# One-core decoder layer: the experts' gates multiply the input rows, and the second product runs in two-part form into one PSUM sum

## The chip, the core and the metric

The kernel runs on one core of a Trainium2 chip. The metric is the time of one execution on the device, in microseconds (us). Engines are named as in the profile: PE (TensorE, with PEld for its weight loads), DVE (VectorE), ACT (ScalarE), POOL (GpSimd) and SP (SyncE, which issues most transfers).

## The reference

One decoder layer on x of shape (4, 256, 128), in three parts, each added to x. Self attention has 16 heads and a causal mask, on 8 sequences of 128 in its own setup (here 4 of 256). Cross attention has 16 heads of 8 on a context of 4 x 256 rows. The part that changes is the mixture of 8 experts, of which each row uses 2:

```
scores = x @ Wr + br                     # 128 -> 8, x is the layer-normalised row
weights = softmax over the best two scores, 0 elsewhere
for i in range(8):
    h = relu(xi @ W1[i] + b1[i])         # 128 -> 512, xi = x where expert i is chosen, else 0
    out += (h @ W2[i] + b2[i]) * weights[..., i:i+1]    # 512 -> 128
```

## The kernel before

**Order.** A table `slots` is written out once in Python. Each engine walks it and emits its own part of every unit, so one row of the table sets the order on all engines, and semaphores do the rest. Every engine works strictly in that order: a wait in one unit holds back all later units of that engine.

**Stages.** First the self attention (`S`, `T`, `V`, `Z`). Then the cross attention: for each batch b of four, eight slots g with two score products (`CS`), whose exponentials ACT writes (`cross_probabilities`, L930), and the value products (`CO`, L718). Beside them run the maxima that a later batch needs (`MX` on PE L682, reduced on DVE L1128), their turn and stacking (`mT`, `stack_m`), and the way out of the batch before (`oq0`, `oT0`, `oq1`, `oT1`, `wo`). All of these small steps share PSUM bank 7 and go one after another. In the slots of batch 2 stands also `WS`: ACT rounds one expert's first weights to fp32r (`weight_high`, L948), and DVE writes the remainder (`weight_low`, L1157).

**Experts.** The 1024 rows go in two halves of 512, and each half meets 8 experts, so there are 16 periods k. In each, PE forms the hidden values in four chunks (`H`, helper `products`, L530 to L532): a product of fp32 accuracy in two-part form, high x high, low x high, high x low, three fp32r products of 512 columns. ACT and DVE take turns in adding the bias b1, applying relu and writing `hid` in fp32 (L953 and L1201). Then `Y` (`combine`, L792) forms the second product of the period before with plain fp32 products: 4 groups of 128 rows x 4 chunks, `hid` being the stationary operand and `w2` the moving one with 128 columns. DVE multiplies each result by the row's gate and adds it to `resid` (`accumulate`, L1220). `NT`, `RT`, `GT`, `WT`, `B2` are the turn of the normalised rows, the router's scores, the gates, their turn and the bias b2.

**Transfers.** SP issues the expert weights in the cross stage: w1 (L389), the stacked maxima of batch 2 (`stack_m(2)`, six small transfers), w2 (L392), then `stack_m(3)`. They all go through one queue.

## Time and profile before

| | |
|---|---|
| Runs | 337.38, 337.92, 335.69 us; median 337.38 us |
| Profiled execution | 336.25 us, of which the span is 334.5 us |
| Busy share of the span | PE 92%, DVE 58%, ACT 49%, POOL 20% |
| Mean granted TensorE clock | 0.995 |
| Last quarter of the cross attention with batch 2 and 3 | 189.8 to 220.6 us |
| Experts | 220.6 to 330.6 us |

The page's shares are means over stages that differ. A PE record's duration includes the time in which the next product already runs, so the price of a product in a stream is the distance between starts.

### The profile page before, as it was taken

To read this page: it belongs to the slowest core of one execution; us is meant where nothing else is said; L and a number is where in the kernel's file an instruction comes from. 1 tells how busy PE (TensorE), PEld (TensorE's weight loads), DVE (VectorE), ACT (ScalarE), POOL (GpSimd) and SP (SyncE) were. 2 spreads that over 40 slices of the span, in tenths; PEclk is the share of its full clock that TensorE was granted. 3 is DMA by queue.
4 is the path that set the end of the run, shared out by engine and by line. 5 is a ranking of instruction groups with operands and counts; after the bars stand their busy time and mean duration, and the time that the engine had idled before them with its cause. 6 is when DMAs were issued, how large, how long until landed. Compare 5 with 4: busy or idle time off the path is not lost.

```text
span 334.5 us, 5887 instructions
## 1 busy us (share of the span) xinstructions
PE 306.4 (92%) x2177; PEld 230.3 (69%) x2194; DVE 193.5 (58%) x450; ACT 163.4 (49%) x466; POOL 66.3 (20%) x102
## 2 busy tenths in 40 slices
PE   6789999999989898889687879899999999999995
PEld 2577677867866676556334333378999988998995
DVE  3677565457297875772877883363553564434432
ACT  1679767487646663663565778742212121212210
POOL 7991470301031003620300203020020000000000
PEclk9999999999999999999999997999999999999999
DMA  8800025511000100010016720000000001000001
GB/s 237 199 2 1 3 39 66 64 21 35 15 2 0 39 11 1 3 29 23 1 35 230 213 81 3 2 2 0 2 0 2 0 3 32 0 2 0 2 0 31
DMA packets 13884, 11.98 MB, mean 36 GB/s; under 512 B 2616, under 2 KB 10912, under 8 KB 13856
## 3 DMA queue, kind: packets, MB, share of 16 engines
q1 hardware_dynamic: 12272, 10.81, 13.6%
q10 hardware_dynamic: 1584, 0.80, 0.9%
q8 instruction: 17, 0.28, 0.4%
q14 instruction: 11, 0.09, 0.1%
HBM read 7.84 MB, written 0.52 MB: 25 GB/s over the span
## 4 chain that ended last, share of the span: by engine, by line
PE 76%; DVE 15%; issue 3%; ACT 3%; POOL 2%; DMA 1%; another core or an unknown queue 0%; DVEq 0%; ACTq 0%; POOLq 0%
PE ps L792 17%; PE ps L530 7%; PE ps L531 7%; PE ps L532 7%; PE ps L604 6%; PE ps L637 5%; PE ps L649 4%; DVE mneg L1128 4%; PE ps L682 4%; PE ps L718 4%; PE ps L703 3%; PE ps L611 2%; PE ps L639 2%; DVE negmax L1097 2%; DVE t_lo L1063 2%
## 5 line engine op out<-in xcount | busy, mean ns | idle before, releaser
L901 ACT ACTIVATE p<-ps,negmax 128x256 f32<-128x256 f32 (+1 forms) x128 | 52.6, 425 | 25.4 <-DVE negmax L1097 24.9
L792 PEld LDWEIGHTS ps<-w_raw,hid 128*128 128x128 f32 x512 | 59.5, 192 | 1.3
L792 PE MATMUL ps<-w_raw,hid 128*128 128x128 f32 x512 | 59.6, 275 | 0.0
L953 ACT ACTIVATE hid<-ps,b1T 128x512 f32<-128x512 f32 x32 | 21.9, 687 | 73.9 <-PE ps L532 73.9
L1128 DVE TENSOR_REDUCE mneg<-ps 128x2 f32<-128x512 f32 x64 | 42.1, 682 | 14.0 <-PE ps L682 13.3
L1097 DVE TENSOR_REDUCE negmax<-ps 128x2 f32<-128x512 f32 (+1 forms) x48 | 32.9, 686 | 19.6 <-PE ps L606 12.4
L930 ACT ACTIVATE px<-ps 128x512 f32<-128x512 f32 x64 | 35.3, 600 | 18.1 <-PE ps L703 15.1
L1220 DVE SCALAR_TENSOR_TENSOR resid<-ps,wgt,resid 128x128 f32<-128x128 f32 x64 | 18.0, 344 | 42.9 <-PE ps L792 42.9
L682 PE MATMUL ps<-k_st,q_mem 128*128 128x256 bf16 x128 | 24.7, 276 | 9.4 <-DVE mneg L1128 8.7
L1201 DVE TENSOR_SCALAR hid<-ps,b1T 128x512 f32<-128x512 f32 x32 | 23.8, 749 | 11.0 <-PE ps L532 10.9
L424 POOL TENSOR_SCALAR tmp<-mv 128x2 f32<-128x2 f32 x8 | 2.1, 268 | 141.2 <-DVE mv L1121 141.2
L887 ACT CAST t_hi<-ps 128x512 fp32r<-128x512 f32 x32 | 18.7, 591 | 19.6 <-PE ps L532 18.7
L530 PE MATMUL ps<-n_parts,w_hi 128*128 128x512 f32 x64 | 27.6, 431 | 0.0
L901 ACT ACTIVATION_READ_ACCUMULATOR p<-ps,negmax 128x1 f32 x128 | 26.6, 208 | 0.0
L532 PE MATMUL ps<-n_parts,w_hi 128*128 128x512 f32 x64 | 25.3, 396 | 0.0
L531 PE MATMUL ps<-n_parts,w_lo 128*128 128x512 f32 x64 | 25.3, 395 | 0.0
L682 PEld LDWEIGHTS ps<-k_st,q_mem 128*128 128x128 bf16 x128 | 9.4, 97 | 21.3 <-DVE mneg L1128 16.8
L604 PE MATMUL ps<-t_hi,n_parts 128*128 128x512 f32 x64 | 23.1, 441 | 0.3 <-DVE t_lo L1063 0.3
L1063 DVE TENSOR_TENSOR t_lo<-ps,t_hi 128x512 fp32r<-128x512 f32 x32 | 21.4, 681 | 1.9 <-ACT t_hi L887 1.9
L703 PE MATMUL ps<-q_mem,k_st 128*128 128x512 bf16 x56 | 20.4, 398 | 0.3 <-ACT px L930 0.2
L530 PE MATMUL ps<-n_parts,g_hi 128*128 128x256 f32 x64 | 20.6, 322 | 0.0
L637 PE MATMUL ps<-p,v_sb 128*64 128x256 f32 x128 | 20.1, 392 | 0.4 <-DVE v_sb L1109 0.4
...
## 6 DMA issues: line engine op xcount, KB each, us to landing
w_raw<-in_L_ffn_W SPq DMA_DIRECT2D x1, 2048.0 KB, 8.5
...
p<-in_L_attn_W_o SPq DMA_DIRECT2D x1, 512.0 KB, 8.0
p<-in_ctx SPq DMA_DIRECT2D x1, 512.0 KB, 9.2
```

The lines of the kernel that those rows point to most:

```text
L530: pe.matmul(out, a[0], b_[0], start=True, stop=False)
L531: pe.matmul(out, a[1], b_[0], start=False, stop=False)
L532: return pe.matmul(out, a[0], b_[1], start=False, stop=True)
L604: pe.matmul(bank, n_parts[:, a, S * b:S * b + P], t_ring[t][:, 2 * (u % 6):2 * (u % 6) + 2, :], start=(a + t == 0), stop=False)
L637: last = pe.matmul(o, v, p0[:, h, :], start=True, stop=False)
L682: last = pe.matmul(ps[:, max_bank[("MX", b, u)], S * par:S * par + S], q_st[b][:, g, S * par + P * qt:S * par + P * qt + P], k_st[:, g, S ...
L703: pe.matmul(ps[:, k % 3, :], k_st[:, g, S * b + P * kt:S * b + P * kt + P], q_st[b][:, g, :], start=True, stop=True).then_inc(s_st, 1)
L792: last = pe.matmul(ps[:, Y_BANK[k % 2], P * tt:P * tt + P], hid[:, k % 2, c, P * tt:P * tt + P], w2_sb[:, NC * e + c, :], start=(c == 0), ...
L901: last = act.activation(dst, bank[:, n * i:n * i + n], ACT.Exp, bias=negmax[:, kt, h:h + 1], accum_out=psums[:, kt, h:h + 1])
L930: act.activation(px[:, (g // 2) % 2, c0:c0 + 512], ps[:, k % 3, :], ACT.Exp, scale=SCALE_X).then_inc(s_px, 1)
L1097: dve.tensor_reduce(dst, ps[:, k % 3, :].rearrange("p (h q) -> p h q", h=n), AX, ALU.max, negate=True).then_inc(s_max, 1)
L1128: dve.tensor_reduce(mneg[:, qt, :].rearrange("p (r g) -> p r g", r=2)[:, :, g], ps[:, max_bank[("MX", b, u)], :].rearrange("p (h k) -> p h ...
```

## The change

The gate is at least 0, so gate x relu(x W1 + b1) = relu((gate x) W1 + gate b1). The changed kernel multiplies the input rows by the gate instead of the result:

- `X` (`gate_rows`) is a new PE product that spreads the gate of expert e over 128 partitions. DVE multiplies the turned rows `nT` by it (`gated`), ACT writes the high part (`gated_high`), DVE the low part (`gated_low`). It stands one period ahead: `X` of k+1 opens the slot of period k.
- The biases b1 and br go into the last row of the weights: a normalised row sums to 0, so its last element is replaced by 1 and the last weight row is subtracted from the others. POOL does so for w1 (`first_weights`, 8 pieces), and it needs `w1_last`, the last row of every expert's w1 repeated on all partitions (2 MB in SBUF), and b1 must land in row 127 of w1 after w1 did. `weight_high` now waits for both.
- All four relu chunks go through ACT (high part) and then DVE (low part).
- `Y` has the weights as stationary operand and moves 512 rows, in two-part form: 4 chunks x 3 fp32r products, and all experts of a half sum up in one PSUM bank. `accumulate` is gone. The sum is copied by ACT (`YE`), turned by PE (`YO`) and added to `resid` by DVE (`finish_rows`), and the output leaves in four parts, not two.
- w2 is split too: ACT writes the high part (`second_high`), POOL the low part (`second_weights`).
- b2 is one product per half. `NT`, `RT`, `GT`, `WT` and `X` of the first half stand in the slots of batch 3 of the cross attention, where before `NT` and `RT` did.

On ACT, in the cross stage, this is the first stretch with `WS` before (p and px are probabilities, w_hi the rounded weights, oT and m_f small steps):

```order
L939 COPY o_raw<-ps 128x512 [waits s_pv]
L948 CAST w_hi<-w_raw 128x512 [waits s_w1]
L930 ACTIVATE px<-ps 128x512 [waits s_pv,s_st] x2
L964 COPY b1T<-ps 128x32 [waits s_misc]
L948 CAST w_hi<-w_raw 128x512 [waits s_w1]
L930 ACTIVATE px<-ps 128x512 [waits s_pv,s_st] x2
```

and now:

```order
L1025 COPY o_raw<-ps 128x512 [waits s_pv]
L1035 CAST w_hi<-w_raw 128x512 [waits s_b1,s_wdiff]
L1016 ACTIVATE px<-ps 128x512 [waits s_pv,s_st] x2
L1035 CAST w_hi<-w_raw 128x512 [waits s_b1,s_wdiff]
L1016 ACTIVATE px<-ps 128x512 [waits s_pv,s_st] x2
```

The place is the same, the wait is another: for b1's transfer and POOL's difference. Later on ACT, in batch 3, stands a new wait for the router's scores:

```order
L1060 COPY nT<-ps 128x512 [waits s_misc]
L1016 ACTIVATE px<-ps 128x512 [waits s_pv,s_st] x2
L1057 ACTIVATE gate<-gate 128x4 [waits s_score]
L1016 ACTIVATE px<-ps 128x512 [waits s_pv,s_st] x4
L1029 COPY oT<-ps 128x128 [waits s_misc]
```

On SP the transfers of the experts now stand so (m_part are the stacked maxima, of batch 2 and then of batch 3):

```order
L409 DMA w_raw<-in_L_ffn_W 128x8x512 [waits s_misc]
L411 DMA w_last<-in_L_ffn_W 128x8x512
L415 DMA b_sb<-in_L_ffn_b 8x128 [waits s_zero]
L415 DMA b_sb<-in_L_ffn_b 8x128
L398 DMA q_mem<-m_part 1x8x256 [waits s_mpart]
L398 DMA q_mem<-m_part 1x8x256 x5
L417 DMA w_raw<-in_L_ffn_W 128x32x128
L419 DMA w_raw<-in_L_ffn_b 1x4096 [waits s_w1]
L398 DMA q_mem<-m_part 1x8x256 [waits s_mpart]
```

The broadcast (L411) is new between w1 and the maxima, and b1 (L419) stands behind w2. The diff, cut to its core:

```diff
-            more = {(2, 1): [("b1", 0)], (3, 1): [("NT", 0)], (3, 7): [("RT", 0)]}
+            more = {(3, 0): [("NT", 0)], (3, 1): [("RT", 0)], (3, 3): [("GT", 0), ("W2", 0, 0)], (3, 5): [("W2", 0, 1)],
+                    (3, 6): [("WT", 0)], (3, 7): [("X", 0)]}
...
-        extra = {0: [("GT", 0), ("oq0", last)], 1: [("WT", 0), ("oT0", last)], 2: [("B2", 0), ("oq1", last)], 3: [("oT1", last), ("wo", last)],
-                 5: [("NT", 1)], 6: [("RT", 1)], 7: [("GT", 1)], 8: [("WT", 1)], 9: [("B2", 1)]}
+        beside = {(0, 0): [("oq0", last)], (0, 1): [("oT0", last)], (0, 2): [("oq1", last)], (0, 3): [("oT1", last)],
+                  (1, 0): [("wo", last)], (3, 1): [("NT", 1)], (4, 0): [("RT", 1)], (5, 1): [("GT", 1)],
+                  (6, 3): [("WT", 1)], (9, 0): [("YO", 0, 0)], (9, 1): [("YO", 0, 1)]}
         for k in range(2 * NE):
-            more = extra.get(k, []) + [None, None]
-            units = [("H", k, 0), more[0], ("H", k, 1), ("H", k, 2), more[1], ("H", k, 3)]
-            slots.append([u for u in units if u] + ([("Y", k - 1)] if k else []))
-        slots.append([("Y", 2 * NE - 1)])
-        MISC = ("PJ", "n2T", "q", "mT", "oq0", "oT0", "oq1", "oT1", "wo", "b1", "NT", "RT", "WT", "B2")
+            slot = [("YE", 0, 0), ("YE", 0, 1)] if k == NE + 1 else []
+            slot += [("X", k + 1)] if k + 1 < 2 * NE else []
+            for c in range(NC):
+                slot += [("H", k, c)] + beside.get((k, c), [])
+            if k + 2 < NE:
+                slot += [("W2", 0, k + 2)]
+            if k % NE == 2:
+                slot += [("B2", k // NE)]
+            slots.append(slot + ([("Y", k - 1)] if k else []))
+        slots.append([("Y", 2 * NE - 1), ("YE", 1, 0), ("YE", 1, 1), ("YO", 1, 0), ("YO", 1, 1)])
...
+        X_BANK = 6
...
-        G_BANK, H_BANK, Y_BANK = (0, 1, 2, 7), (0, 1, 2, 5), (6, 3)
+        G_BANK, H_BANK, Y_BANK = (0, 1, 2, 7), (0, 1, 2, 5), (3, 4)
...
-            sp.dma_start(b1_nat[:, :], b1.rearrange("e (c p) -> (e c) p", p=P)).then_inc(s_ffnb, 16)
...
             sp.dma_start(w1_raw[:, :].rearrange("p (e n) -> p e n", n=HID), w1.rearrange("e p n -> p e n")
                          ).then_inc(s_w12[0], 16)
+            sp.dma_start(w1_last[:, :].rearrange("p (e n) -> p e n", n=HID), w1[:, LAST, :].partition_broadcast(P)
+                         ).then_inc(s_wlast, 16)
+            sp.wait_ge(s_zero, 1)
+            for r in (0, LOW):
+                sp.dma_start(b2_sb[r:r + NE, :], b2).then_inc(s_b2, 16)
             stack_m(2)
-            sp.dma_start(w2_sb, w2.rearrange("e (c p) d -> p (e c) d", p=P)).then_inc(s_w12[1], 16)
+            sp.dma_start(w2_raw[:, :].rearrange("p (n d) -> p n d", d=D), w2.rearrange("e (c p) d -> p (e c) d", p=P)).then_inc(s_w12[1], 16)
+            sp.wait_ge(s_w12[0], 16)
+            sp.dma_start(w1_raw[LAST:D, :], b1.rearrange("e n -> (e n)").unsqueeze(0)).then_inc(s_b1, 16)
             stack_m(3)
...
-                sp.wait_ge(s_acc, NE * (hf + 1))
-                sp.dma_start(out.rearrange(tiles, p=P)[:, 4 * hf:4 * hf + 4, :],
-                             resid[:, 4 * hf:4 * hf + 4, :]).then_inc(s_out, 16)
-            sp.wait_ge(s_out, 32)
+                for i in range(2):
+                    ts = slice(4 * hf + 2 * i, 4 * hf + 2 * i + 2)
+                    sp.wait_ge(s_misc_ev, misc_at[("YO", hf, i)] + 1)
+                    sp.dma_start(out.rearrange(tiles, p=P)[:, ts, :], resid[:, ts, :]).then_inc(s_out, 16)
...
+            def first_weights(i):
+                if i == 0:
+                    pool.wait_ge(s_w12[0], 16)
+                    pool.wait_ge(s_wlast, 16)
+                cols = slice(512 * i, 512 * i + 512)
+                pool.tensor_tensor(w1_raw[0:LAST, cols], w1_raw[0:LAST, cols], w1_last[0:LAST, cols], ALU.subtract
+                                   ).then_inc(s_wdiff, 1)
+            def second_weights(i):
+                pool.wait_ge(s_w2hi, i + 1)
+                cols = slice(512 * i, 512 * i + 512)
+                pool.tensor_tensor(w2_lo[:, cols], w2_raw[:, cols], w2_hi[:, cols].bitcast(F32), ALU.subtract
+                                   ).then_inc(s_w2lo, 1)
...
+            for i in range(NE):
+                first_weights(i)
             norm_3(0)
             norm_3(1)
             norm_3(2)
+            for i in range(3):
+                second_weights(i)
             norm_3(3)
+            for i in range(3, NE):
+                second_weights(i)
...
                 elif kind == "RT":
+                    pe.wait_ge(s_pick, 3)
                     for t in ts:
-                        for i in range(2):
-                            last = pe.matmul(ps[:, 7, NE * (t % 4):NE * (t % 4) + NE],
-                                             n_parts[:, i, P * t:P * t + P].bitcast(F32), wr_sb[:, :],
-                                             start=(i == 0), stop=(i == 1))
+                        last = pe.matmul(ps[:, 7, NE * (t % 4):NE * (t % 4) + NE], nT[:, P * t:P * t + P], wr_sb[:, :],
+                                         start=True, stop=True)
...
+            def gate_rows(k):
+                e, hf = k % NE, k // NE
+                if k == 0:
+                    pe.wait_ge(s_mx_ev, 16 * B)
+                if e == 0:
+                    pe.wait_ge(s_misc_ev, misc_at[("WT", hf)] + 1)
+                ge(pe, s_xf, k)
+                pe.matmul(ps[:, X_BANK, :], pick[:, e, :], wgtT[:, 512 * hf:512 * hf + 512], start=True, stop=True
+                          ).then_inc(s_gt, 1)
             def hidden(k, c):
-                e, hf = k % NE, k // NE
+                e = k % NE
                 if k == 0 and c == 0:
                     pe.wait_ge(s_wlo, 8)
                     pe.wait_ge(s_px, 16 * B)
                     pe.wait_ge(s_mx_ev, 16 * B)
-                if k % NE == 0 and c == 0:
-                    pe.wait_ge(s_misc_ev, misc_at[("NT", hf)] + 1)
+                if c == 0:
+                    pe.wait_ge(s_xlo, k + 1)
                 if k >= 1:
-                    pe.wait_ge(s_ha if c % 2 == 0 else s_hd, 2 * (k - 1) + c // 2 + 1)
-                products(ps[:, H_BANK[c], :], [w[:, e, P * c:P * c + P] for w in w1_p], n_of(512 * hf, 512)).then_inc(s_h, 1)
+                    pe.wait_ge(s_hd, 4 * (k - 1) + c + 1)
+                products(ps[:, H_BANK[c], :], [w[:, e, P * c:P * c + P] for w in w1_p],
+                         [x[:, k % 2, :] for x in x_p]).then_inc(s_h, 1)
             def combine(k):
-                e = k % NE
+                e, hf = k % NE, k // NE
+                out_bank = ps[:, Y_BANK[hf], :]
+                pe.wait_ge(s_w2lo, e + 1)
                 if k == 0:
-                    pe.wait_ge(s_w12[1], 16)
                     pe.wait_ge(s_pv_ev, 2 * B)
-                ge(pe, s_acc, k - 1)
-                pe.wait_ge(s_ha, 2 * k + 2)
-                pe.wait_ge(s_hd, 2 * k + 2)
-                for tt in range(4):
-                    for c in range(NC):
-                        last = pe.matmul(ps[:, Y_BANK[k % 2], P * tt:P * tt + P], hid[:, k % 2, c, P * tt:P * tt + P],
-                                         w2_sb[:, NC * e + c, :], start=(c == 0), stop=(c == NC - 1))
+                for c in range(NC):
+                    pe.wait_ge(s_hd, 4 * k + c + 1)
+                    w, h = [w[:, NC * e + c, :] for w in w2_p], [x[:, k % 2, c, :] for x in hid]
+                    pe.matmul(out_bank, w[0], h[0], start=(e == 0 and c == 0), stop=False)
+                    pe.matmul(out_bank, w[1], h[0], start=False, stop=False)
+                    last = pe.matmul(out_bank, w[0], h[1], start=False, stop=(e == NE - 1 and c == NC - 1))
                 last.then_inc(s_y, 1)
+            def second_bias(hf):
+                pe.wait_ge(s_b2, 32)
+                pe.matmul(ps[:, Y_BANK[hf], :], b2_sb[:, :], wgtT[:, 512 * hf:512 * hf + 512].bitcast(F32),
+                          start=False, stop=False)
...
             def weight_high(i):
-                act.wait_ge(s_w12[0], 16)
+                act.wait_ge(s_wdiff, i + 1)
+                act.wait_ge(s_b1, 16)
                 act.copy(w1_hi[:, 512 * i:512 * i + 512], w1_raw[:, 512 * i:512 * i + 512]).then_inc(s_whi, 1)
-            def relu(k, c):
+            def second_high(i):
+                act.wait_ge(s_w12[1], 16)
+                act.wait_ge(s_wdiff, NE)
+                act.copy(w2_hi[:, 512 * i:512 * i + 512], w2_raw[:, 512 * i:512 * i + 512]).then_inc(s_w2hi, 1)
+            def gated_high(k):
+                act.wait_ge(s_xf, k + 1)
+                ge(act, s_h, 4 * (k - 1))
+                act.copy(x_p[0][:, k % 2, :], x_f[:, k % 2, :]).then_inc(s_xhi, 1)
+            def relu_high(k, c):
                 act.wait_ge(s_h, 4 * k + c + 1)
                 ge(act, s_y, k - 1)
-                act.activation(hid[:, k % 2, c, :], ps[:, H_BANK[c], :], ACT.Relu,
-                               bias=b1T[:, NC * (k % NE) + c:NC * (k % NE) + c + 1]).then_inc(s_ha, 1)
-            def expert_copy(kind, hf):
+                act.activation(hid[0][:, k % 2, c, :], ps[:, H_BANK[c], :], ACT.Relu).then_inc(s_ha, 1)
...
+                    act.wait_ge(s_y, NE * (hf + 1))
+                    ge(act, s_misc, misc_at[("YO", hf - 1, i)] + 1 if hf else 0)
+                    half_cols = slice(S * i, S * i + S)
+                    act.copy(yT[:, half_cols], ps[:, Y_BANK[hf], half_cols]).then_inc(s_yT, 1)
...
-            def relu(k, c):
-                dve.wait_ge(s_h, 4 * k + c + 1)
-                ge(dve, s_y, k - 1)
-                dve.tensor_scalar(hid[:, k % 2, c, :], ps[:, H_BANK[c], :], b1T[:, NC * (k % NE) + c:NC * (k % NE) + c + 1],
-                                  0.0, ALU.add, ALU.max).then_inc(s_hd, 1)
...
+            def gated(k):
+                hf = k // NE
+                dve.wait_ge(s_gt, k + 1)
+                ge(dve, s_xhi, k - 1)
+                dve.tensor_tensor(x_f[:, k % 2, :], ps[:, X_BANK, :], nT[:, 512 * hf:512 * hf + 512], ALU.mult
+                                  ).then_inc(s_xf, 1)
+            def gated_low(k):
+                dve.wait_ge(s_xhi, k + 1)
+                dve.tensor_tensor(x_p[1][:, k % 2, :], x_f[:, k % 2, :], x_p[0][:, k % 2, :].bitcast(F32), ALU.subtract
+                                  ).then_inc(s_xlo, 1)
+            def relu_low(k, c):
+                dve.wait_ge(s_ha, 4 * k + c + 1)
+                dve.scalar_tensor_tensor(hid[1][:, k % 2, c, :], ps[:, H_BANK[c], :], 0.0,
+                                         hid[0][:, k % 2, c, :].bitcast(F32), ALU.max, ALU.subtract).then_inc(s_hd, 1)
+            def finish_rows(hf, i):
+                dve.wait_ge(s_misc, misc_at[("YO", hf, i)] + 1)
                 dve.wait_ge(s_n3, 4 * hf + 4)
-                ge(dve, s_acc, accumulated(hf))
-                dve.tensor_tensor(resid[:, ts, :], ps[:, 7, :].rearrange("p (t d) -> p t d", d=D),
+                ts = slice(4 * hf + 2 * i, 4 * hf + 2 * i + 2)
+                dve.tensor_tensor(resid[:, ts, :], ps[:, turn_bank(hf, i), 0:S].rearrange("p (t d) -> p t d", d=D),
                                   resid[:, ts, :], ALU.add).then_inc(s_misc_ev, 1)
-                dve.wait_ge(s_misc_ev, misc_at[("B2", hf)] + 1)
-            def accumulate(k):
-                e, hf = k % NE, k // NE
-                dve.wait_ge(s_y, k + 1)
-                dve.wait_ge(s_n3, 4 * hf + 4)
-                ge(dve, s_acc, k)
-                for tt in range(4):
-                    t = 4 * hf + tt
-                    last = dve.scalar_tensor_tensor(resid[:, t, :], ps[:, Y_BANK[k % 2], P * tt:P * tt + P],
-                                                    wgt[:, t, e:e + 1], resid[:, t, :], ALU.mult, ALU.add)
-                last.then_inc(s_acc, 1)
...
+                    elif kind == "H":
+                        relu_low(b, *i)
+                        if i[0] == 0 and b + 1 < 2 * NE:
+                            gated_low(b + 1)
+                    elif kind == "X":
+                        gated(b)
+                        if b == 0:
+                            gated_low(b)
```

## Rows read from the trace of the kernel before

**Rows 1.** Windows: busy us of each engine, granted clock, DMA share, GB/s.
```profile
189.80:204.10 14.30, 10.95 (x87) 4.97 (x88) 11.87 (x29) 11.44 (x25) 0.71 (x2) 0.95 0.37 100
220.60:330.60 110.00, 109.71 (x766) 99.09 (x762) 50.95 (x151) 24.39 (x40) 2.06 (x5) 1.00 0.01 3
```

**Rows 2.** Timeline, end of the experts: start us, us, engine line op.
```profile
320.91 0.39 PE L532 MATMUL ps<-n_parts,w_hi 128*128 128x512 f32 x1
...
323.01 0.39 PE L532 MATMUL ps<-n_parts,w_hi 128*128 128x512 f32 x1
...
327.01 1.13 DVE L1220 SCALAR_TENSOR_TENSOR resid<-ps,wgt,resid 128x128 f32<-128x128 f32 x4 [2.82 <-PE ps L792]
330.59 1.13 DVE L1220 SCALAR_TENSOR_TENSOR resid<-ps,wgt,resid 128x128 f32<-128x128 f32 x4 [2.45 <-PE ps L792]
331.74 0.37 SPq L396 DMA_DIRECT2D out_dram<-resid  x1
```

**Rows 3.** Page, costliest groups: busy us, mean ns, idle before.
```profile
L953 ACT ACTIVATE hid<-ps,b1T 128x512 f32<-128x512 f32 x32 | 21.9, 687 | 73.9 <-PE ps L532 73.9
L1063 DVE TENSOR_TENSOR t_lo<-ps,t_hi 128x512 fp32r<-128x512 f32 x32 | 21.4, 681 | 1.9 <-ACT t_hi L887 1.9
```

**Rows 4.** Timeline, router and gates of the first half.
```profile
217.86 1.85 PE L755 MATMUL ps<-wr_sb,n_parts 128*128 128x8 f32 x16
...
219.75 0.19 DVE L1170 COPY score<-ps 128x32 f32<-128x32 f32 x1 [2.29 <-PE ps L755]
...
221.78 0.16 DVE L1184 CAST top_f<-top_i 128x8 f32<-128x8 uint32 x1
221.90 0.20 ACT L960 ACTIVATE gate<-gate 128x4 f32<-128x4 f32 x1 [2.96 <-DVE gate L1179]
...
223.49 0.19 DVE L1195 TENSOR_TENSOR wgt<-hot 128x32 f32<-128x32 f32 x1
```

**Rows 5.** Page, DMA issues: count, KB each, us from issue to landing.
```profile
w_raw<-in_L_ffn_W SPq DMA_DIRECT2D x1, 2048.0 KB, 8.5
...
p<-in_ctx SPq DMA_DIRECT2D x1, 512.0 KB, 9.2
...
wx<-in_L_xattn_Wq SPq DMA_DIRECT2D x1, 64.0 KB, 8.7
...
w_raw<-in_L_ffn_W SPq DMA_DIRECT2D x1, 0.5 KB, 11.2
```

**Rows 6.** Timeline of SP's issues: start us, us.
```profile
3.40 0.43 SPq L341 DMA_DIRECT2D p<-in_ctx  x1
3.88 2.78 SPq L343 DMA_DIRECT2D wx<-in_L_xattn_Wq  x1
...
177.21 0.45 SPq L389 DMA_DIRECT2D w_raw<-in_L_ffn_W  x1
...
185.59 0.85 SPq L392 DMA_DIRECT2D w_raw<-in_L_ffn_W  x1
```

**Rows 7.** Windows of PE: its busy us, granted clock, DMA share, GB/s.
```profile
182.00:184.00 2.00, 1.32 (x10) 1.00 1.04 406
```

**Rows 8.** Windows of SP: granted clock, DMA share, GB/s.
```profile
187.00:194.60 7.60, 1.00 0.97 273
```

**Rows 9.** Timeline, batches 2 and 3 of the cross attention.
```profile
189.82 0.62 ACT L948 CAST w_hi<-w_raw 128x512 fp32r<-128x512 f32 x1
...
196.31 0.39 PE L691 MATMUL ps<-ident,mneg 128*16 128x128 f32 x2 [0.54 <-ACT oT L943]
...
199.81 1.08 ACT L930 ACTIVATE px<-ps 128x512 f32<-128x512 f32 x2
...
204.14 0.15 PEld L703 LDWEIGHTS ps<-q_mem,k_st 128*128 128x128 bf16 x1 [0.28 <-DMA q_mem<-m_part]
```

**Rows 10.** Timeline of POOL, splitting the keys.
```profile
39.40 2.13 POOL L310 TENSOR_TENSOR o_raw<-k_f,k_part 128x1024 f32<-128x1024 f32 x1
```

**Rows 11.** Windows of PE, end of batch 2: busy us, granted clock, DMA share, GB/s.
```profile
202.50:206.00 3.50, 3.50 (x28) 0.51 0.01 2
```

189 lines of the change are left out of this document (110 added, 79 removed).

## The prediction

> **What bounds the kernel now.** I read the table of stages first. From 220.6 to 330.6 us PE is busy for 109.7 of 110.0 us at full clock, while DVE has 51 and ACT 24 us of work [rows 1]: the experts are bound by PE alone, so what PE issues there is the price. From 189.8 to 204.1 us, with the weights being rounded, no engine is full, but ACT is busy for 11.4 of 14.3 us and DVE for 11.9 [rows 1], and all walk one order: a wait put into ACT there is soon everyone's. Then I read the timeline of one period for prices, and the transfers for what ACT will wait for.
>
> **The periods.** In a stream of fp32r products of 512 columns, nine starts take 2.10 us (320.91 to 323.01, one expert's hidden chunks 2 to 4) [rows 2], 0.233 each; twelve are 2.80 us. The second product ends 3.58 us after the one before it where nothing stands between (327.01 to 330.59) [rows 2]. It becomes 12 fp32r products, 2.80 us, so 0.78 us less; the new gate product adds 0.23. Each period gains 0.55 us, sixteen gain **8.8 us**.
>
> By the Trainium skill (TensorE: Matmul & The Clock Gate, "Back-to-back issue gap") a product of 512 columns takes N / 2.4 + 2.5 ns = 0.216 us at full clock; by that estimate the new period would be 25 x 0.216 = 5.4 and not 5.8 us, and the whole some 5 us faster still. The rows at full clock say 0.233 and decide.
>
> **Who could be late in a period.** A new period is 5.83 us. DVE has six passes over 512 columns (gate, low part of the rows, four relu parts) at 0.68 us [rows 3]: 4.1 us. ACT has five at 0.69 [rows 3], 3.4 us, and one more of these for w2 in the first periods. Both fit, and PE reads a chunk only a period later. In the first period there is no such lead. PE finishes `oq0` at 1.5 us of it, but DVE has the gate product of the next rows, the first relu part and the low rows ahead of it, each behind a pass of ACT: it ends them at about 3.65 (0.3 + 5 x 0.68), and the normalisation, three small steps of the size of those on `score` and `wgt` (0.2 each, [rows 4]), at 4.3. `oT0` therefore waits from 2.2 to 4.3, and `oT1` for another 0.9: **+3.0 us**. In the second half's `RT` and `GT` DVE has 1.9 (219.75 to just before 221.78) and 1.9 us more (221.78 to 223.68) [rows 4], plus two new steps of 0.2 for the gates' parts, against a spare of 1.7 us per period: `RT` fits with ACT's wait in it, `GT` leaves relu parts late by **0.9 us**. Bounds for both together: 0 (all waits hidden by PE's queue) and 6.
>
> **Small products.** The router has 8 records where it had 16 that took 1.85 us [rows 4]: 0.92 less, twice. The result of the first half must be turned, four products as in `oq0`, 0.6. b2, `NT` and `WT` I leave at their price. Sum **-1.2 us**.
>
> **The first half's gates.** They move into batch 3. ACT's exponential for the gates waits for DVE's 2.1 us of maxima after the scores (219.75 to 221.90) [rows 4], with the scores' own products before them, while ACT's next two exponentials, 1.08 us [rows 9], stand behind it. PE can run one slot ahead, so of some 1.6 us idle ACT part is caught up; the turn of the gates adds 0.6 on PE. At the end, `X` for k = 0, ACT's high and DVE's low part stand before the first `H`, 0.23 + 3 x 0.68, beside `CO`, about what `RT` and `CO` took before. I take **+1.3**, between 0 (slack) and 3 (all of it).
>
> **The end.** After the last product stood DVE's 1.13 us [rows 2]. Now come ACT's copy of 256 columns twice, two transposes and DVE's addition: 2 x 0.4 + 0.3 + 0.5 and three handoffs, 1.8. **+0.7**, 0 to 1.5.
>
> **The wait in the cross stage** is the largest term. ACT takes its first `w_hi` at 189.82 [rows 9], 4 us after w1 landed (177.21 + 8.5) [rows 5, 6]. It will stand behind b1. SP's queue serves its transfers one behind the other: Wq, 64 KB, was issued at 3.88 and took 8.7 us, and so landed at 12.6, exactly when the 512 KB of ctx did that was issued ahead of it (3.40 + 9.2) [rows 5, 6]. So:
> - w1 lands at 185.7 as now.
> - `w1_last` writes another 2 MB. At the pace of w1, of whose 8.5 us about 1 went before bytes moved, 7.5 us: 193.2. `stack_m(2)` stands behind it; the scores of batch 2 wait for it from 189, and the wait lies inside the next one.
> - w2 kept the DMA engines 97% busy for 7.6 us [rows 8]: 200.8.
> - b1 is a mere 16 KB, but behind w2: about 201, and POOL's first difference is done long before (1,024 columns take 2.13 us [rows 10], 508 about 1.1).
>
> ACT's first `w_hi` starts at 200.8 and not at 189.8: 11.0 us. Meanwhile PE can go on for a slot and then stops. How much is caught up? From `w_hi` to the turn of batch 3's maxima (189.82 to 196.31) ACT has 3 x 0.62, 6 x 0.54 and 0.28 of work, 5.4 of 6.5 us: 1.0 us is won. From that turn to the first scores of batch 3 (204.14) the maxima must be split, issued and landed, and today these scores wait for the landing [rows 9], so the 7.8 us between are fixed. Then PE's clock: after the thin stretch of today it was granted 0.51 of 2.4 GHz, so 1.2 GHz, from 202.5 to 206.0 [rows 11]; idle for 8 us it will fall for once more, where ACT is the slower anyway: +0.5. Together **+10.5 us**. The Trainium skill (DMA: Bandwidth & Descriptors, "Queues, rings and completion order") says that a completion is counted only after all earlier writes of that DMA engine; this agrees with the pair at 12.6 us.
>
> **The sum**, against the profiled execution (336.25 us, span 334.5): -8.8 + 3.9 - 1.2 + 1.3 + 0.7 + 10.5 = +6.4, so 342.6. That execution lay 1.1 us below the median of 337.38 and inside the runs; I put the median of the changed kernel at **343 us**, 1.7% slower.
>
> **Rivals.**
> 1. **ACT is not held (ends faster).** The place is ACT's first `w_hi`. If the broadcast, which reads one row of 2 KB for all partitions, passes quickly, and b1's few bytes overtake w2, the weights are ready by 191 and the term is 0 to 1: 336.25 - 8.8 + 3.9 - 1.2 + 1.3 + 0.7 + 0.7 = 332.8. Release at 194.4 is where gain and loss balance. For it: b1 needs no byte of w2, and nothing in the profile shows a broadcast of this size. Against: the landing pair of the start.
> 2. **The transfers are held but move at the best rate.** Two MB at the 406 GB/s seen for 2 us [rows 7] take 5.2 us each: three of them, from 178.3 on (w1's issue and about 0.6 to its first bytes), end at 193.9, with b1 and its landing 194.6, a term of +4.3: 336.4. Against: w2 ran at 273 over its whole length [rows 8]. The Trainium skill (DMA: Bandwidth & Descriptors, "Anatomy of one DMA") gives bytes / 436 GB/s + 2 us, by which three times 2 MB from 177.7 would be done at an estimated 194.1, and the sum be 336. The rows of w2 speak against it.
> 3. **The broadcast is slow.** Half as slow again as w1, since all engines read the same bytes: +3.7, 346.5; double, 350.
> 4. **The handoffs bind.** If a chain of PE, ACT and DVE, not PE, sets the period at 6.4 us as before, the 8.8 us are gone: 351. DVE would have to lose 1.7 us in each period to POOL's `second_weights` or to waits.
>
> **How the numbers follow.** Chances: forecast 0.50 (339 to 346), rival 1 0.17, rival 2 0.14, rival 3 0.12, rival 4 0.07. The range leaves out most of rival 1 and of rival 4: 334 to 349. About 1% (334.0 to 340.7) is what a measurement of this kernel can tell from no change. Faster: rival 1 and a share of rival 2, 0.18. The same: the rest of rival 2 and the lower edge of the forecast, 0.24. Slower: 0.58.
>
> **What would show it.** `w_hi` first at about 201, with ACT and PE idle before it, and b1's transfer landing after w2; periods of 5.8 us between the gate products; PE idle for 2 to 3 us in the first period; a gap on ACT before the gates' exponential. The forecast falls if the first `w_hi` stands before 195, or if periods are above 6.1 us.

## The result and the profile after

The changed kernel took 348.4 us (median of 4 runs, 346.6 to 350.3), the kernel before 336.9 beside it (4 runs): ratio 1.034, 95% interval 1.027 to 1.041. It is slower by 11.5 us; 343 were forecast, 334 to 349 the range, so the result lies 0.6 us under the range's upper edge. The profiled execution took 347.81 us, span 346.0 (before: 336.25 and 334.5).

The places of the forecast come first. SyncE's (SP's) transfers (start, duration in the queue's issue, line), answering to [rows 6]:

```profile
179.66 0.45 SPq L409 DMA_DIRECT2D w_raw<-in_L_ffn_W  x1
180.15 0.57 SPq L411 DMA_DIRECT2D w_last<-in_L_ffn_W  x1
180.77 3.94 SPq L415 DMA_DIRECT2D b_sb<-in_L_ffn_b  x2
184.75 4.08 SPq L398 DMA_DIRECT2D q_mem<-m_part  x6
189.39 0.85 SPq L417 DMA_DIRECT2D w_raw<-in_L_ffn_W  x1
190.30 7.76 SPq L419 DMA_DIRECT2D w_raw<-in_L_ffn_b  x1
211.09 4.11 SPq L398 DMA_DIRECT2D q_mem<-m_part  x6
```

The page's transfers, last column the us to landing, answering to [rows 5]:

```profile
w_raw<-in_L_ffn_W SPq DMA_DIRECT2D x1, 2048.0 KB, 8.6
w_last<-in_L_ffn_W SPq DMA_DIRECT2D x1, 2048.0 KB, 14.5
...
w_raw<-in_L_ffn_W SPq DMA_DIRECT2D x1, 0.5 KB, 12.9
```

The first matrix lands at 188.3, the broadcast at 194.7, the second matrix at 202.3. What waits for them, from the timelines of PE, POOL and ACT, answering to [rows 9]:

```profile
196.22 0.61 PE L765 MATMUL ps<-q_mem,k_st 128*128 128x512 bf16 x1 [5.58 <-DMA q_mem<-m_part]
204.62 0.39 PE L744 MATMUL ps<-k_st,q_mem 128*128 128x256 bf16 x2 [2.77 <-DVE mneg L1233]
208.76 0.39 PE L753 MATMUL ps<-ident,mneg 128*16 128x128 f32 x2 [0.54 <-ACT oT L1029]
```

```profile
194.81 10.28 POOL L519 TENSOR_TENSOR w_raw<-w_raw,w_last 127x512 f32<-127x512 f32 x8 [26.24 <-DMA w_last<-in_L_ffn_W]
```

```profile
202.36 0.62 ACT L1035 CAST w_hi<-w_raw 128x512 fp32r<-128x512 f32 x1 [2.17 <-DMA w_raw<-in_L_ffn_b]
```

Read them in order of time: PE first waits 5.6 us for 24 KB of maxima that stand in SP's queue behind the broadcast; then ACT waits for the bias row, which stands behind the second matrix; then PE for DVE, whose maxima stand behind the low parts of ACT's late splits. The windows of the stage (busy us of PE, PEld, DVE, ACT and POOL, granted clock, DMA share, GB/s), answering to [rows 1]:

```profile
189.80:204.10 14.30, 5.90 (x35) 2.05 (x34) 4.67 (x8) 4.62 (x9) 9.29 (x8) 0.76 0.82 228
190.00:200.00 10.00, 4.42 (x28) 1.55 (x27) 2.19 (x5) 2.49 (x5) 5.19 (x5) 0.66 1.05 286
```

In the first of them PE did 5.9 us of work against 11.0 before, DVE 4.7 against 11.9 and ACT 4.6 against 11.4. In the experts the gate products open the periods (268.42 and 274.20 are two of them), and PE waits for DVE in several places:

```profile
236.02 0.47 PE L592 MATMUL ps<-x_hi,w_hi 128*128 128x512 f32 x1 [0.84 <-DVE x_lo L1309]
239.56 0.33 PE L794 MATMUL ps<-ident,o_n 128*128 128x128 f32 x1 [1.48 <-DVE o_n L1249]
242.55 0.33 PE L794 MATMUL ps<-ident,o_n 128*128 128x128 f32 x1 [0.83 <-DVE o_n L1249]
```

```profile
268.42 0.40 PE L841 MATMUL ps<-wgtT,pick 128*128 128x512 f32 x1
274.20 0.40 PE L841 MATMUL ps<-wgtT,pick 128*128 128x512 f32 x1
277.39 0.51 PE L592 MATMUL ps<-x_hi,w_hi 128*128 128x512 f32 x1 [1.40 <-DVE hid_lo L1314]
...
297.63 0.44 PE L829 MATMUL ps<-ident,o_raw 128*128 128x128 f32 x2 [1.99 <-DVE resid L1321]
```

An undisturbed period is 274.20 - 268.42 = 5.78 us. The wait at 297.63 has a tail; the window behind it has the clock in its third column from the end:

```profile
298.40:301.80 3.40, 3.40 (x10) 2.66 (x9) 1.51 (x3) 1.19 (x2) 0.00 (x0) 0.50 0.29 82
```

At 0.50, that is 1.2 GHz, eight products start in the 3.40 us from 298.37 to 301.77; at the full clock they take 0.23 us each, 1.84 in all, so 1.6 us is lost.

**The ledger of the two profiled spans** (346.0 - 334.5 = 11.5 us):

| stretch | before | after | difference | forecast |
|---|---|---|---|---|
| to the issue of the first matrix | 177.21 | 179.66 | +2.45 | 0 |
| from there to the issue of the fourth batch's maxima | 21.44 | 31.43 | **+9.99** | +10.5 |
| from there to the first hidden product | 21.99 | 24.93 | +2.94 | +1.3 |
| experts, to the end of the last product | 109.95 | 105.76 | -4.19 | -6.1 |
| behind the last product | 3.91 | 4.22 | +0.31 | +0.7 |

The first row has three parts. 1.0 us stands there already at 160 us: in this execution the clock was 0.71 from 135 to 140 us (1.00 before), in code that both kernels share. 1.1 us comes from the change: DVE's copy of the second batch's maxima takes 1.77 us beside GpSimd's clearing of the new buffers (after, after, before):

```profile
164.68 1.77 DVE L332 CAST m_part<-m_r 16x256 bf16<-16x256 f32 x1
165.32 0.94 POOL L540 MEMSET wgtT<- 128x1024 f32 x1
```

```profile
163.69 0.70 DVE L311 CAST m_part<-m_r 16x256 bf16<-16x256 f32 x1
```

The rest, 0.4 us, stands behind it, where the clock was low once more (windows of PE, after and before):

```profile
168.00:172.00 4.00, 4.00 (x24) 1.57 (x24) 2.75 (x7) 1.67 (x3) 0.56 (x3) 0.58 0.03 6
```

```profile
168.00:172.00 4.00, 2.97 (x26) 1.28 (x26) 3.90 (x9) 1.91 (x4) 0.00 (x0) 1.00 0.08 21
```

### The profile page after: what moved, and what is told of

The parts are those of the page before. It is cut to its first block, busy times and chain, and to the rows that moved or that the text cites. A ratio compares the mean times of both kernels' runs of the same rounds, so it can differ in the third digit from the quotient of the medians.

```text
span 346.0 us, 5393 instructions
## 1 busy us (share of the span) xinstructions
PE 301.5 (87%) x1852; PEld 212.2 (61%) x1869; DVE 214.7 (62%) x452; ACT 190.4 (55%) x525; POOL 91.2 (26%) x130
## 4 chain that ended last, share of the span: by engine, by line
PE 65%; DVE 16%; DMA 4%; ACT 4%; issue 3%; SPq 3%; POOL 2%; another core or an unknown queue 0%; DVEq 0%; ACTq 0%; POOLq 0%
PE ps L592 6%; PE ps L594 6%; PE ps L593 6%; PE ps L666 6%; PE ps L699 4%; PE ps L711 4%; PE ps L868 4%; PE ps L869 4%; PE ps L870 4%; DMA w_raw<-in_L_ffn_b 3%; PE ps L744 3%; DVE mneg L1233 3%; PE ps L780 3%; PE ps L673 2%; PE ps L701 2%
## 5 line engine op out<-in xcount | busy, mean ns | idle before, releaser
L1314 DVE SCALAR_TENSOR_TENSOR hid_lo<-ps,hid_hi 128x512 fp32r<-128x512 f32 x64 | 41.8, 685 | 23.3 <-ACT hid_hi L1051 23.3
L1051 ACT ACTIVATE hid_hi<-ps 128x512 fp32r<-128x512 f32 x64 | 35.0, 596 | 8.1 <-PE ps L594 7.6
L744 PE MATMUL ps<-k_st,q_mem 128*128 128x256 bf16 x128 | 25.5, 283 | 12.3 <-DVE mneg L1233 11.5
L1046 ACT CAST x_hi<-x_f 128x512 fp32r<-128x512 f32 x16 | 9.9, 620 | 38.8 <-DVE x_f L1304 38.8
L592 PE MATMUL ps<-x_hi,w_hi 128*128 128x512 f32 x64 | 26.4, 412 | 2.2 <-DVE hid_lo L1314 1.4
L868 PE MATMUL ps<-hid_hi,w_hi 128*128 128x512 f32 x64 | 26.4, 412 | 0.0
L594 PE MATMUL ps<-x_lo,w_hi 128*128 128x512 f32 x64 | 25.7, 402 | 0.0
L593 PE MATMUL ps<-x_hi,w_lo 128*128 128x512 f32 x64 | 25.5, 399 | 0.0
L869 PE MATMUL ps<-hid_hi,w_lo 128*128 128x512 f32 x64 | 25.3, 395 | 0.0
L870 PE MATMUL ps<-hid_lo,w_hi 128*128 128x512 f32 x64 | 25.2, 393 | 0.0
```

Source lines behind the costliest of these rows:

```text
L592: pe.matmul(out, a[0], b_[0], start=True, stop=False)
L593: pe.matmul(out, a[1], b_[0], start=False, stop=False)
L594: return pe.matmul(out, a[0], b_[1], start=False, stop=True)
L744: last = pe.matmul(ps[:, max_bank[("MX", b, u)], S * par:S * par + S], q_st[b][:, g, S * par + P * qt:S * par + P * qt + P], k_st[:, g, S ...
L868: pe.matmul(out_bank, w[0], h[0], start=(e == 0 and c == 0), stop=False)
L869: pe.matmul(out_bank, w[1], h[0], start=False, stop=False)
```

## The experiments

Theory 1: the loss is one hold in the cross stage, made of what stands in SP's queue behind the broadcast and the second matrix; the experts gain nearly what was forecast. Rivals: the hold is DMA rate or GpSimd's subtractions, or the small waits elsewhere carry the loss. **Hold** below is the time from the issue of the first matrix to that of the fourth batch's maxima, **batch 4** from there to the first hidden product; ratios are to the kernel before, timed beside each (its medians lie between 336.8 and 337.3 us). In act_turns another queue issues the first matrix, so it has no such hold; rows_112 was run once and has no interval.

| kernel | us (runs) | ratio, 95% interval | hold | batch 4 |
|---|---|---|---|---|
| before | 336.9 (4) | | 21.44 | 21.99 |
| changed | 348.4 (4) | 1.034, 1.027 to 1.041 | 31.43 | 24.93 |
| no_last | 337.5 (10) | 1.000, 0.996 to 1.003 | 21.44 | 24.86 |
| before_last | 343.5 (5) | 1.020, 1.017 to 1.022 | 27.99 | 21.18 |
| split_b3 | 346.6 (4) | 1.026, 1.023 to 1.030 | 28.28 | 28.76 |
| bias_first | 424.4 (5) | 1.258, 1.254 to 1.263 | 109.08 | 24.96 |
| rows_112 | 349.2 (1) | | 33.84 | 24.95 |
| pool_late | 348.1 (4) | 1.030, 1.024 to 1.036 | 33.43 | 24.93 |
| turn_later | 344.7 (4) | 1.024, 1.021 to 1.028 | 30.90 | 24.94 |
| order_mid | 346.9 (4) | 1.031, 1.027 to 1.035 | 31.39 | 25.10 |
| order_spread | 343.9 (4) | 1.021, 1.017 to 1.025 | 24.04 | 31.43 |
| act_last | 339.0 (10) | 1.005, 1.002 to 1.007 | 25.24 | 24.95 |
| act_turns | 340.2 (6) | 1.010, 1.006 to 1.013 | | 24.93 |
| best | 332.5 (6) | 0.986, 0.984 to 0.989 | 21.91 | 24.68 |

### The hold taken away: no_last

```diff
-            sp.dma_start(w1_last[...], w1[:, LAST, :].partition_broadcast(P))
...
-            sp.wait_ge(s_w12[0], 16)
-            sp.dma_start(w1_raw[LAST:D, :], b1...)
...
-            for i in range(NE):
-                first_weights(i)
...
-                act.wait_ge(s_wdiff, i + 1)
-                act.wait_ge(s_b1, 16)
+                act.wait_ge(s_w12[0], 16)
...
-                act.wait_ge(s_wdiff, NE)
```

> The changed kernel without the broadcast of the matrix's last row, without GpSimd's subtraction of it and without the bias row (these parts of the computation are left out); ACT's w_hi waits for the first matrix alone, as in the kernel before. It measures what the three cost together. Theory 1 (the cross stage's wait of 10.1 us is all theirs): first expert product near 225.5 us, total 337 to 339 us. Rival (half of the wait is the second matrix's and the maxima's own): 342 to 344.

337.5 us, 10.9 less than the changed kernel, and the hold is 21.44, as before to the hundredth. The first hidden product starts at 223.41. The place of the loss is thereby settled, for the three parts together. Its size is 10.0 us by the rows, where 10.5 were forecast; the 10.9 of the medians is less exact, since the ten runs lie between 333.6 and 338.8. The batch behind it is as long as in the changed kernel (24.86), so its 2.9 us are not the hold's. And GpSimd clears its buffers here too, while DVE's copy takes 0.70 us and the first matrix is issued at 177.11: the clearing does not always cost something.

### The broadcast alone, in the kernel before: before_last

```diff
             sp.dma_start(w1_raw[...], w1...)
+            sp.dma_start(w1_last[...], w1[:, LAST, :].partition_broadcast(P)).then_inc(s_wlast, 16)
             stack_m(2)
             sp.dma_start(w2_sb, ...)
```

> The kernel before with one transfer more: the 2 MB broadcast of the first matrix's last row, behind the first matrix as in the changed kernel; nothing reads it. Theory 1 (in-order queue): the stacked maxima of the third batch land behind it, near 196, and PE waits 5 to 6 us for them; nothing else is held, so 342 to 343.5 us. Rival (the transfer is hidden beside the chain, and only its readers cost something): 337 to 338.

343.5 us: 6.6 more than before, with nobody reading the 2 MB. PE's timeline has one new wait:

```profile
192.28 0.61 PE L707 MATMUL ps<-q_mem,k_st 128*128 128x512 bf16 x1 [5.09 <-DMA q_mem<-m_part]
```

and behind it a stretch at a mean clock of 0.58 (busy us of PE, PEld, DVE, ACT and POOL, then the clock):

```profile
192.00:196.00 4.00, 3.72 (x24) 1.43 (x25) 0.79 (x2) 1.57 (x3) 0.00 (x0) 0.58 1.04 300
```

So the maxima behind the broadcast cost 6.6 us by themselves, the stretch at low clock included. The forecast put this wait inside ACT's longer one and gave it no price of its own; it stays when ACT's is taken away.

### ACT's wait moved away: split_b3

```diff
-                if b == 2:
+                if b == 3:
                     slot += [("WS", 0, g)]
```

> The changed kernel with ACT's and DVE's splits of the first matrix (w_hi, w_lo) moved from the third batch of the cross attention to the fourth; all DMAs and GpSimd's subtractions stay as they are. Theory 1 (ACT is held in its own queue until the bias row and the differences are there, first w_hi at 202.36): that hold is gone, and what stays in the cross stage is the wait of PE for the stacked maxima (5.6 us, until 196.2); the 16 splits lengthen the fourth batch by 0 to 2 us. 342 to 345 us. Rival (the wait for the maxima is all there is, the splits lie beneath it): 347 to 349, and the first expert product stays near 236 us.

346.6 us, worse than expected. The hold falls by 3.15 us to 28.28 (near before_last's 27.99), so ACT's wait is worth that on top of the wait for the maxima; but the eight splits cost the fourth batch 3.8 us (28.76), where 0 to 2 were expected. The time is near the rival's, the mechanism is theory 1's: the time was moved, not won.

### The bias row first: bias_first and rows_112

```diff
-            sp.dma_start(w1_raw[:, :]..., w1...)
+            sp.dma_start(w1_raw[0:LAST, :]..., w1[:, 0:LAST, :]...)
+            sp.dma_start(w1_raw[LAST:D, :], b1...).then_inc(s_b1, 16)
             sp.dma_start(w1_last[...], ...)
...
             sp.dma_start(w2_raw[...], ...)
-            sp.wait_ge(s_w12[0], 16)
-            sp.dma_start(w1_raw[LAST:D, :], b1...)
```

> The changed kernel, but rows 0 to 126 of the first matrix and the bias row are fetched by two transfers, one right behind the other, so that the bias row waits for nothing and stands ahead of the broadcast and of the second matrix. Theory 1 (the bias row, issued at 190.3 behind the second matrix and 7.8 us in issue, is what ends ACT's hold at 202.36): the first w_hi now waits for GpSimd's first difference alone, at 196.1, so 5 to 6 us of the 10 come back: 342 to 344 us. Rival (the differences, 1.28 us each on GpSimd against 0.6 on ACT, or the maxima bind next): no more than 2 us come back, 346 to 348.

424.4 us: neither theory. SP's timeline and a window inside it:

```profile
178.36 0.41 SPq L409 DMA_DIRECT2D w_raw<-in_L_ffn_W  x1
178.82 74.98 SPq L411 DMA_DIRECT2D w_raw<-in_L_ffn_b  x1
```

```profile
200.00:220.00 20.00, 0.00 (x0) 0.00 (x0) 0.00 (x0) 0.00 (x0) 0.00 (x0) 0.50 0.07 26
```

The DMA share is 0.07, one engine of sixteen, and 26 GB/s: the transfer of 127 rows ran on one engine. SP could not even issue the next one for 75 us. rows_112 tests the count of rows: 112 and 15 in place of 127.

> The changed kernel with rows 0 to 126 of the first matrix in two transfers, 112 and 15 rows, and the bias row right behind. In the run with one transfer of 127 rows the DMA engines stood at a share of 0.07, 26 GB/s, for over 70 us. Theory 1 (127 rows, which 16 does not divide, go to one engine, 112 go to sixteen, 7 each): the 112 rows (1.8 MB) land in about 8 us at 250 to 400 GB/s; the 15 rows (240 KB) are the short ones: under 2 us if spread, 9 us at 26 GB/s if they go to one engine. 343 to 352 us. Rival (it was the bias row of 16 KB, or the number of transfers, that held the queue): 420 us again.

349.2 us (one run), and the 75 us are gone; the 112 rows land 10.5 us after their issue and the 15 rows 12.1 us after theirs. While they move, the windows show 251 and 174 GB/s at a DMA share above 1 (the last two columns), so the split costs something, and the maxima are held for 9.4 us instead of 5.6:

```profile
184.00:188.00 4.00, 3.27 (x26) 1.96 (x29) 3.27 (x11) 2.49 (x6) 0.00 (x0) 1.00 1.06 251
188.00:192.00 4.00, 2.23 (x20) 0.67 (x12) 3.14 (x6) 1.52 (x3) 0.00 (x0) 1.00 1.08 174
```

The row count was the cause. The Trainium skill (DMA: Bandwidth & Descriptors, "Why a DMA increments its semaphore by 16 and not by 1") states it: a transfer is spread over the largest number of engines, up to 16, that divides the slowest dimension on both of its sides, and 127 partitions give one engine. This case's 0.07 and 26 GB/s agree. The bias row's place was thus not tested by this kernel; order_mid did that.

### GpSimd's clearing later: pool_late

```diff
             norm_2(3)
             pool.wait_ge(s_misc, misc_at[("PJ", B - 1)] + 1)
+            pool.wait_ge(s_mpart, 6)
+            pool.wait_ge(s_qpart, 12)
```

> The changed kernel, in which GpSimd waits for DVE's splits of the second batch's maxima and of the last queries before it clears the new buffers (at 165 to 169 us now, beside those splits). Theory 1 (the clearing holds DVE's bf16 copy of the maxima, 1.77 us at 164.7 against 0.3 otherwise, and PE behind it by 2.4 us): the first matrix is issued near 178 instead of 179.7, and 1.0 to 2.2 us come back: 346 to 347.4. Rival (the stretch is late for a reason of its own): 348.4, and the copy still takes over 1 us.

348.1 us, above what was expected: no gain that the runs can tell (345.7 to 349.3, the changed kernel 346.6 to 350.3). The first half came as expected: DVE's copy of the maxima takes 0.70 us instead of 1.77 and the first matrix is issued at 177.86. But the hold grew to 33.43. What the clearing costs can be read from the other profiles, which all have it at its old place but meet it differently. In five of them (the changed kernel, split_b3, rows_112, order_spread, best) the copy takes 1.77 us and PE waits 2.43 us behind it; in the six others the copy takes 0.70 to 0.84 and PE waits 1.33 to 1.48 (1.34 in the kernel before). So it costs about 1 us in some executions, and it is not what the 11.5 us are made of.

### The turn of the result later: turn_later

```diff
-                  ... (9, 0): [("YO", 0, 0)], (9, 1): [("YO", 0, 1)]}
+                  ... (9, 0): [("YO", 0, 0)], (9, 3): [("YO", 0, 1)]}
```

> The changed kernel with the second turn of the first half's result two hidden products later ((9, 3) instead of (9, 1)). Theory 1 (PE waits 2.0 us at 297.6 for DVE's sum of the first turn, which stands behind other work on DVE, and then runs 4 us at a clock of 0.78): that wait and the slow stretch behind it go, 345 to 346.5 us. Rival (the wait only moves to the next step that bank 7 or DVE holds): 348.4.

344.7 us, 3.7 less than the changed kernel, where 1.9 to 3.4 were expected (the intervals of the two ratios just touch, so the size is not sure). PE's wait is 0.58 instead of 1.99 us, and no window behind it is below full clock:

```profile
295.12 0.44 PE L829 MATMUL ps<-ident,o_raw 128*128 128x128 f32 x2 [0.58 <-DVE resid L1321]
```

So a wait of 2 us that the forecast does not have was worth 3 in the changed kernel's profile: 1.4 of waiting and 1.6 of the clock behind it. The second part is not always there. Eight of the profiled kernels have this wait, 1.97 to 1.99 us; in four (the changed kernel, split_b3, pool_late, act_last) the 3.4 us behind it ran at 0.51 to 0.56, in the four others (no_last, rows_112, order_mid, order_spread) at 1.00.

### The queue in another order: order_mid and order_spread

```diff
-            sp.dma_start(w1_last[...], ...)
...
             stack_m(2)
-            sp.dma_start(w2_raw[...], ...)
             sp.wait_ge(s_w12[0], 16)
             sp.dma_start(w1_raw[LAST:D, :], b1...)
+            sp.dma_start(w1_last[...], ...)
+            sp.dma_start(w2_raw[...], ...)
             stack_m(3)
```

> The changed kernel with its transfers in another order: first matrix, second biases, stacked maxima of the third batch, then (once the first matrix is there) the bias row, then the broadcast of the last row, then the second matrix. The splits stay in the third batch. Theory 1 (the queue works in order, so what stands behind the 2 MB broadcast waits for it): the stacked maxima land with the first matrix, near 188.4, and PE's wait of 5.6 us for them is gone; the bias row is no longer behind the second matrix; the broadcast lands near 197 and ACT's first w_hi comes near 198.5, 4 us earlier than at 202.4: 343 to 345 us. Rival (the bias row's issue takes 7 us wherever it stands, and the broadcast starts behind it): first w_hi at 203 or later, 347 to 349.

346.9 us: missed, though the profiled execution is the fastest of the four (343.9). The first half of the mechanism held: the wait for the maxima is gone, the bias row's issue takes 0.23 us instead of 7.76, and ACT's first split starts at 197.28. But it came to nothing, because ACT and PE now wait for GpSimd's first difference, and through DVE for the splits:

```profile
197.28 0.62 ACT L1035 CAST w_hi<-w_raw 128x512 fp32r<-128x512 f32 x1 [7.37 <-POOL w_raw L519]
```

```profile
199.68 0.61 PE L744 MATMUL ps<-k_st,q_mem 128*128 128x256 bf16 x2 [8.11 <-DVE mneg L1233]
```

The hold is 31.39, as before this edit: two waits in a row, for the maxima and for the splits, were one longer wait. The first split does start 20.1 us after the issue of the first matrix, instead of 22.7. But DVE's second `w_lo` now takes 1.78 us beside GpSimd, and the clock from 200 to 210 is 0.75, where the changed kernel has 1.00.

order_spread adds to that order the splits from step 5 of the third batch on, the second matrix behind the fourth batch's maxima, and its first two splits some steps later:

> As the run with the transfers in another order, and besides: the splits of the first matrix in the last three steps of the third batch and the first five of the fourth, the second matrix fetched behind the maxima of the fourth batch and its first two splits some steps later. Theory 1 (the 10 us of the cross stage are the hold alone, as the run without the broadcast shows, which came out at 337.5): nothing is held, five splits more in the fourth batch cost 1 to 2 us: 338 to 340. Rival (the splits cost the fourth batch as much as they did when all eight stood there, 3.8 us by the first expert product at 235.2 with the second-batch stage 4.6 us shorter): 341 to 343.

343.9 us, beyond even the rival's 343. The hold is down to 24.04, the fourth batch up to 31.43. DVE's timeline has the reason:

```profile
197.46 0.62 DVE L329 CAST m_part<-m_f 16x256 bf16<-16x256 f32 x1 [1.14 <-ACT m_f L1003]
198.11 1.37 DVE L331 TENSOR_TENSOR m_r<-m_f,m_part 16x256 f32<-16x256 f32 x1
199.52 1.24 DVE L332 CAST m_part<-m_r 16x256 bf16<-16x256 f32 x1
200.79 1.36 DVE L334 TENSOR_TENSOR m_part<-m_r,m_part 16x256 bf16<-16x256 f32 x1
```

Beside GpSimd's subtractions (196.66 to 207.0, 1.29 us each) the four take 4.7 us from start to end; in order_mid, where the second to fourth stand behind GpSimd's last, 1.6. Each now lasts about as long as one subtraction. Reductions from PSUM between them keep their 0.68. The Trainium skill (SBUF — State Buffer, "Who interferes with whom") has a rule for it: DVE and GpSimd share one pair of ports, under an exclusive lock; a DVE operation with two inputs in SBUF, or a fast copy or cast, contends with GpSimd for it, and a reduction does not. These rows agree: 1.24 to 1.37 us for the last three steps against 0.28 to 0.41, and no change for the reductions.

### Another queue: act_last and act_turns

```diff
+                        if (b, *i) == (0, 5, 1):
...
+                            act.dma_start(w1_last[...], w1[:, LAST, :].partition_broadcast(P))...
```

> The changed kernel with the 2 MB broadcast issued by ScalarE's queue, after the exponents of step 5 of the first cross batch (near 171), while the DMA engines are at a share of 0.1 to 0.2; the bias row stands on SyncE's queue before the second matrix. Nothing else moves. Theory 1 (the hold comes from what stands in line behind the broadcast and behind the second matrix): the maxima of the third batch and the bias row land by 190, GpSimd's differences begin with the first matrix, near 186, and nothing is held but DVE's two-input operations that meet GpSimd's subtractions: first expert product at 224 to 226, 338 to 340 us. Rival (the differences on GpSimd, 10.3 us for eight, hold DVE so far that 4 us or more stay): 342 to 344.

339.0 us (10 runs): as expected, 9.4 less than the changed kernel, with everything computed. The broadcast is issued by ACT at 162.59 (I had put this step near 171), when the engines are free, and lands in 8.7 us. What stays of the hold, 3.8 us, is read from the rows as DVE beside GpSimd: its first `w_lo` takes

```profile
192.01 1.76 DVE L1264 TENSOR_TENSOR w_lo<-w_raw,w_hi 128x512 fp32r<-128x512 f32 x1
```

instead of 0.68 (the second 1.78), PE waits 1.67 us for DVE next, and the clock from 190 to 200 is 0.83. act_turns puts the first matrix on ACT's queue as well and moves the turns of the experts:

> As the run with the broadcast on ScalarE's queue, with the first matrix too on that queue right behind it (both there near 183), the first half's second result turn at (9, 3), and the turns of the last cross outputs at (0, 2), (1, 1), with the product behind them at (1, 3), instead of (0, 1), (0, 3), (1, 0). Theory 1 (hold, turn wait and first-period waits are all separate and all go): 337.5 for the kernel without the hold, less 3 for the turn, less 1.5 to 2 for the first period, plus 1 for DVE beside GpSimd: 333.5 to 336, a little below the kernel before. Rival (what is freed goes into other waits and a lower clock): 338 to 341.

340.2 us: the rival's. GpSimd's subtractions now come at 178.60 to 188.9 and meet DVE's splits of the third batch's maxima, whose three later steps take 4.0 us; they are issued at 187.82, 5.7 us later than in act_last, and the first hidden product starts at 232.48 instead of 227.42. From there to the end it takes 3.7 us less than act_last (106.3 against 110.0), which is what the turns' new places give.

### All of it: best

> All that the runs have shown, in one kernel: the broadcast on ScalarE's queue as in the run with it alone (339.0); the eight splits of the first matrix from step 2 of the third batch to step 1 of the fourth, so that DVE's w_lo (1.76 us there instead of 0.68) does not meet GpSimd's subtractions; the second result turn of the first half at (9, 3); the turns of the last cross outputs at (0, 2), (1, 1) and (1, 3); the first two splits of the second matrix behind x_hi of the first product instead of ahead of it, and the gates of the second half at (5, 3) instead of (5, 1), so that GpSimd's w_lo does not meet DVE's x_lo and one-hot rows. Theory 1 (each of these waits was its own): 339.0 less 3.7 (turn), 1 to 1.5 (first period), 1 to 2 (w_lo and the dip of the clock behind it), 0.5 (x_lo), 1 (gates): 330.5 to 333, faster than the kernel before by 1 to 2 %. Rival (as in the run with both transfers on ScalarE's queue, half of what is freed comes back as other waits): 334.5 to 336.5, within 1 % of it.

```diff
...
-                if b == 2:
-                    slot += [("WS", 0, g)]
+                if 0 <= 8 * (b - 2) + g - 2 < NE:
+                    slot += [("WS", 0, 8 * (b - 2) + g - 2)]
...
```

332.5 us, ratio 0.986 (0.984 to 0.989): faster than the kernel before by 1.4% and than the change by 4.6%, and within theory 1's range. It changes several things at once and does not part them. `w_lo` is back at 0.68, the hold at 21.91, and the windows are at full clock from the stage to the end:

```profile
198.56 0.68 DVE L1264 TENSOR_TENSOR w_lo<-w_raw,w_hi 128x512 fp32r<-128x512 f32 x1
```

```profile
190.00:200.00 10.00, 8.86 (x78) 3.87 (x79) 7.76 (x16) 7.49 (x15) 9.63 (x12) 1.00 0.76 211
200.00:227.00 27.00, 20.20 (x178) 9.75 (x171) 15.62 (x58) 20.72 (x44) 6.77 (x15) 1.00 0.01 2
227.00:332.00 105.00, 98.74 (x438) 78.07 (x436) 65.90 (x133) 48.41 (x95) 11.96 (x14) 1.00 0.02 6
```

## Why the prediction was right, and where its size was off

The direction and the main term were right: the experts' gain is real, and the hold in the cross stage eats it. The size was too small: +6.4 us were forecast, +11.5 measured. By the ledger's rows the 5.1 us between them are +2.45 ahead of the stage, -0.5 in the hold, +1.6 in the fourth batch, +1.9 in the experts and -0.4 at the end. The result lies outside the forecast's own span (339 to 346). That it still lies in the range is in part luck: the upper part of the range was there for a slow broadcast, and that did not come. By the terms:

- **The hold, +10.5: measured 10.0 by the rows.** The chain was forecast as w1, broadcast, w2, bias row at 201; it was released at 202.36 with the issue 2.45 us late, so 22.7 us after the issue of w1 where 23.6 was forecast. That is 0.9 us too long, and the 1.0 us of catching up is 0.9 too much (from `w_hi` to the turn of the maxima it is 6.40 us after and 6.49 before): the two errors cancel by luck. The 0.5 us for the clock did not come in the stretch. The wait for the maxima lies inside ACT's, as forecast, since order_mid takes it away and wins nothing; what the working lacks is that it would cost 6.6 us by itself (before_last), so that no repair of the bias row's wait alone could win more than about 3 us. Rivals 1 to 3 are out. The bias row did not overtake: its issue alone took 7.76 us. The transfers did not move at the best rate: the window from 190 to 200 shows 286 GB/s. The formula that the prediction takes there from the Trainium skill is, by that section's heading, the one for transfers that GpSimd issues; these are SyncE's. And the broadcast was not slow: it landed 15.0 us after the issue of w1 (16.0 forecast), and in act_last it took 8.7 us from issue to landing, about as w1 does. GpSimd's pieces are 512 columns, not 508, and take 1.29 us, not 1.1; in the changed kernel that binds nothing, in order_mid it does.
- **The periods, -8.8:** 5.78 us against 5.83 forecast. Rival 4 is out. The estimate of 5.4 from the Trainium skill is not what the rows show; its section gives the formula for an isolated product, and the difference would come to nearly 7 us over sixteen periods, not 5.
- **DVE late, +3.9:** 1.48 + 0.83 in the first period (3.0 forecast) and 1.40 in the second half's `GT` (0.9). Sum 3.7.
- **Not in the sum: the wait at the turn of the first half's result.** The turn was priced as four products, 0.6 us, and nothing was put down for waiting. PE waits 1.99 us for DVE, since the second turn needs the bank of the first, and loses 1.6 to the clock in this execution. turn_later: 3.7 us.
- **The first half's gates, +1.3: measured +2.9,** in the changed kernel and in no_last alike. This is the term that was mis-sized: `NT` waits 1.03 us for GpSimd's rows (there was no wait before), and `x_lo` takes 1.19 us beside GpSimd's `w_lo` before the first hidden product can start, 0.84 us late. The upper bound of 3 was the right value.
- **The end, +0.7:** measured +0.3.

The sum of the small terms, -4.1, is what no_last should show: 333. Its profiled execution has 333.6, but the median of its ten is 337.5, with mean clocks of 0.98 to 0.99 where the three fastest (333.6, 333.8 and 336.1) have 0.995. The turn's wait is in this kernel too (1.97 us). In the profiled execution full clock follows it, in others of the kernels 3.4 us at about half clock. That the slower executions of no_last differ by such stretches fits their mean clocks; no trace of a slow one is kept, so the 4 us stay unexplained.

Open: why pool_late's hold is 2 us longer than the changed kernel's, though it starts earlier; only the clock (0.83 against 1.00 from 200 to 210) differs in the rows.
